# Dense bursts of four in three of eight half tiles, and the first tile turned two steps earlier

## The reference

```python
def attn(x):                     # 32 heads, KV_LAT = 4, HEAD_DIM = 32
    C_q, C_kv = x @ Wq_d + bq_d, x @ Wkv_d + bkv_d            # 12 and 4 columns
    q = (C_q @ W_qk + b_qk).reshape(b, s, 32, 4)
    scores = einsum('bqhd,bkd->bhqk', q, C_kv) / sqrt(4)
    V = (C_kv @ Wv_u + bv_u).reshape(b, s, 32, 32)
    out = einsum('bhqk,bkhd->bqhd', softmax(scores), V).reshape(b, s, 1024)
    return out @ Wo + bo
def ffn(x):                      # N = 8, RANK = 16
    h = einsum('bsd,nrd->nbsr', x, lora_A)
    return x @ W.T + bias + einsum('nbsr,nor->bso', h, lora_B * 2 * lora_weights)
x = x + attn(layernorm(x))
x = x + ffn(layernorm(x))
```

## Time and profile before

| | us |
|---|---|
| median of 3 runs | 2167.85 |
| the three runs | 2167.52, 2167.85, 2172.3 |
| the profiled execution | 2171.91 |
| its span | 2170.1 |
| preparation, up to the first scores | 137.7 |
| one of the chunks 2 to 6 | 243.0 |
| behind the last scores (2096.4) to the end | 73.7 |

### The profile page before, as it was taken

One profiled execution on the slowest core, in us unless ns is written; L12 is line 12 of the kernel. 1 busy time (PEld: TensorE's weight loads), 2 busy tenths in 40 slices (PEclk: granted clock), 3 DMA queues, 4 the chain that ended last, 5 costly groups with the idle time before them and its releaser, 6 DMA issues. The chain is left out here.

```text
span 2170.1 us, 35966 instructions
## 1 busy us (share of the span) xinstructions
PE 1954.2 (90%) x15023; PEld 717.3 (33%) x15023; DVE 511.2 (24%) x1292; ACT 2005.0 (92%) x2193; POOL 180.3 (8%) x100
## 2 busy tenths in 40 slices
PE   5748888799999999899999999899989999899989
PEld 3412222233333333233333333233333333233337
DVE  8732133212102110212102120212102120212125
ACT  6948999999999999999999999999999999999960
POOL 1210001000100001100100001100100000100111
PEclk9978999999999999999999999999999999999999
DMA  7432201000010000100010000100010000100010
GB/s 239 175 81 87 83 15 35 5 4 25 25 44 6 13 26 25 34 14 14 25 44 6 14 24 25 34 15 13 25 44 6 19 19 25 35 16 14 24 39 39
DMA packets 49116, 78.99 MB, mean 36 GB/s; under 512 B 17790, under 2 KB 33206, under 8 KB 48954
## 3 DMA queue, kind: packets, MB, share of 16 engines
q1 hardware_dynamic: 48954, 76.69, 10.6%
HBM read 52.02 MB, written 24.64 MB: 35 GB/s over the span
## 5 line engine op out<-in xcount | busy, mean ns | idle before, releaser
L554 ACT ACTIVATE probs<-ps 128x1024 f32<-128x1024 f32 x2048 | 1911.5, 1029 | 64.7 <-PE ps L765 37.9
L776 PE MATMUL ps<-probs,c_wide 128*32 128x512 f32 x8192 | 990.6, 601 | 0.0
L765 PE MATMUL ps<-q_in,key_t 30*128 30x512 bf16 x4096 | 405.2, 385 | 146.4 <-ACT probs L554 137.1
L821 PE MATMUL ps<-w_eff,xn_t 128*128 128x512 f32 x1344 | 387.0, 416 | 0.0
L765 PEld LDWEIGHTS ps<-q_in,key_t 30*128 30x128 bf16 x4096 | 103.8, 91 | 766.5 <-ACT probs L554 712.0
L776 PEld LDWEIGHTS ps<-probs,c_wide 128*32 128x32 f32 x8192 | 213.3, 109 | 427.3 <-issue 241.3
L1230 DVE TENSOR_TENSOR y<-ps,y 128x512 f32<-128x512 f32 x64 | 44.3, 692 | 965.2 <-PE ps L821 954.9
L821 PEld LDWEIGHTS ps<-w_eff,xn_t 128*128 128x128 f32 x1344 | 230.4, 188 | 98.5 <-issue 63.5
L460 POOL TENSOR_TENSOR y<-y,ffn_bias 128x1024 f32<-128x1024 f32 x32 | 76.2, 2381 | 1169.4 <-DVE xn L987 1169.4
L456 POOL TENSOR_TENSOR y<-y,attn_bias 128x1024 f32<-128x1024 f32 x32 | 76.2, 2383 | 704.8 <-DMA y<-in_L_attn_x_dram 704.6
L1009 DVE CAST xn_t<-ps 128x512 fp32r<-128x512 f32 x64 | 44.2, 691 | 158.9 <-PE ps L806 158.9
(11 more groups left out here) (130 smaller groups left out, 598.6 us busy)
## 6 DMA issues: line engine op xcount, KB each, us to landing
y<-in_L_attn_x_dram SPq DMA_DIRECT2D x48, 512.0 KB, 4.2
out_dram<-y SPq DMA_DIRECT2D x32, 512.0 KB, 2.7
area<-in_L_attn_x_dram SPq DMA_DIRECT2D x16, 512.0 KB, 4.5
q_in<-q_parts SPq DMA_DIRECT2D x256, 30.0 KB, 1.7
q_parts<-q_parts_sb SPq DMA_DIRECT2D x48, 128.0 KB, 2.1
y<-in_L_attn_Wo_dram SPq DMA_DIRECT2D x1, 2048.0 KB, 8.5
xn<-in_L_attn_Wo_dram SPq DMA_DIRECT2D x1, 2048.0 KB, 13.5
y<-in_L_ffn_W_dram SPq DMA_DIRECT2D x1, 2048.0 KB, 8.0
```

Source lines behind the costliest of these rows:

```text
L554: nc.scalar.activation(probs[:, (c * STEPS + step) % PROBS, bass.ts(pair, 2 * N)], ps[:, 2 * (i % SCORE_SLOTS):2 * (i % SCORE_SLOTS) + 2, ...
L765: last = nc.tensor.matmul(ps[:, at, :], key_t[TILE * h:TILE * h + KEYS, bass.ts(b * KT + kt, P)], q_in[TILE * h:TILE * h + KEYS, g % 2, :] ...
L776: last = nc.tensor.matmul(ps[32 * h:32 * h + 32, SUMS, :], c_wide[:, b * KT + kt, at:at + 32], probs[:, (c * STEPS + step) % PROBS, bass.t ...
L821: last = nc.tensor.matmul(ps[:, SHARED, :], xn_t[:, t % 2, a, kb, :], w_eff[:, b, kb, bass.ts(half, N)], start=(kb + i == 0), stop=(kb == ...
```

## The change

The plan is now computed, from a table of burst sizes per tile and half. Sizes of 4 give six bursts, sizes of 5 give five. The high halves of tiles 0, 1 and 2 have size 4; all others stay at 5. The first tile starts at step 13, which is `FIRST_AT + 6`. The computed steps are:

| tile | first turn | high bursts | next projections | low bursts |
|---|---|---|---|---|
| 0 before | 15 | 19 to 27 | 29, 31 | 33 to 41 |
| 0 after | 13 | 17 to 27 | 29, 31 | 33 to 41 |
| 1 before | 43 | 47 to 55 | 57, 59 | 61 to 69 |
| 1 after | 43 | 47 to 57 | 59, 61 | 63 to 71 |
| 2 before | 73 | 77 to 85 | 87, 89 | 91 to 99 |
| 2 after | 75 | 79 to 89 | 91, 93 | 95 to 103 |
| 3 before | 101 | 105 to 113 | none | 119 to 127 |
| 3 after | 105 | 109 to 117 | none | 119 to 127 |

`TURN_AT` goes from 71 to 73. `STORE_AT` and `LOAD_AT` keep their values.

```diff
-        DENSE_AT = (4, 6, 8, 10, 12, 18, 20, 22, 24, 26)
-        BURSTS = len(DENSE_AT) // 2
-        BURST = -(-3 * KB // BURSTS)
-        NEXT_AT = 14
-        TILE_STEPS = DENSE_AT[-1] + 2
+        BURST = ((4, 5), (4, 5), (4, 5), (5, 5))
+        BURSTS = [[-(-3 * KB // size) for size in sizes] for sizes in BURST]
         TURN_BACK_AT = BEHIND + 3
         FIRST_AT = BEHIND + 5
-        TILE_AT = [15, 15 + TILE_STEPS, 17 + 2 * TILE_STEPS, 17 + 3 * TILE_STEPS]
-        TURN_AT = TILE_AT[2] - 2
-        STORE_AT = [min(-(-(at + TILE_STEPS) // KT), G4 - 1) for at in TILE_AT]
+        TILE_AT, NEXT_AT, DENSE_AT = [], [], []
+        at = FIRST_AT + 6
+        for t in range(TT):
+            if t == 2:
+                TURN_AT = at
+                at += 2
+            TILE_AT.append(at)
+            high = [at + 4 + 2 * j for j in range(BURSTS[t][0])]
+            NEXT_AT.append(high[-1] + 2)
+            low = [high[-1] + 2 + (4 if t < TT - 1 else 0) + 2 * j for j in range(BURSTS[t][1])]
+            DENSE_AT.append((high, low))
+            at = low[-1] + 2
+        TILE_END = [low[-1] + 2 for high, low in DENSE_AT]
+        STORE_AT = [min(-(-at // KT), G4 - 1) for at in TILE_END]
...
             def dense_burst(p, t, half, j):
-                for kb, i in PRODUCTS[BURST * j:BURST * (j + 1)]:
+                size = BURST[t][half]
+                for kb, i in PRODUCTS[size * j:size * (j + 1)]:
...
-                    if at in DENSE_AT:
-                        half, j = divmod(DENSE_AT.index(at), BURSTS)
-                        if j == 0 and half == 0:
-                            pe.wait_ge(t_moved, START + CHUNKS * KB + (p * TT + t + 1) * 2)
-                        elif j == 0 and t < TT - 1:
-                            pe.wait_ge(y_ready, START + (p * TT + t + 2) * 2)
-                        elif j == 0:
-                            pe.wait_ge(ffn_moved, START + (p * TT + t) * 2 + 1)
-                        dense_burst(p, t, half, j)
+                    for half in range(2):
+                        if step in DENSE_AT[t][half]:
+                            j = DENSE_AT[t][half].index(step)
+                            if j == 0 and half == 0:
+                                pe.wait_ge(t_moved, START + CHUNKS * KB + (p * TT + t + 1) * 2)
+                            elif j == 0 and t < TT - 1:
+                                pe.wait_ge(y_ready, START + (p * TT + t + 2) * 2)
+                            elif j == 0:
+                                pe.wait_ge(ffn_moved, START + (p * TT + t) * 2 + 1)
+                            dense_burst(p, t, half, j)
```

More of the change, by code:

```diff
@@ L822, in dense_burst @@
                                             start=(kb + i == 0), stop=(kb == KB - 1 and i == 2))
-                if j == BURSTS - 1:
+                if j == BURSTS[t][half] - 1:
                     last.then_inc(ffn_ready, 1)
@@ L840, in dense_beside @@
                 for t in range(TT):
-                    at = step - TILE_AT[t]
-                    if at == 0:
+                    if step == TILE_AT[t]:
                         if t == 2:
@@ L847, in dense_beside @@
                         turn_xn(p, t, 0, SHARED)
-                    if at == 2:
+                    if step == TILE_AT[t] + 2:
                         pe.wait_ge(t_moved, START + CHUNKS * KB + (p * TT + t) * 2 + 1)
                         turn_xn(p, t, 1, SHARED)
-                    if t < TT - 1 and at == NEXT_AT:
+                    if t < TT - 1 and step == NEXT_AT[t]:
                         pe.wait_ge(ffn_moved, START + (p * TT + t) * 2 + 1)
                         project(p, t + 1, 0, SHARED)
-                    if t < TT - 1 and at == NEXT_AT + 2:
+                    if t < TT - 1 and step == NEXT_AT[t] + 2:
                         pe.wait_ge(y_ready, START + (p * TT + t + 1) * 2 + 1)
                         project(p, t + 1, 1, SHARED)
-                    if at in DENSE_AT:
-                        half, j = divmod(DENSE_AT.index(at), BURSTS)
-                        if j == 0 and half == 0:
-                            pe.wait_ge(t_moved, START + CHUNKS * KB + (p * TT + t + 1) * 2)
-                        elif j == 0 and t < TT - 1:
-                            pe.wait_ge(y_ready, START + (p * TT + t + 2) * 2)
-                        elif j == 0:
-                            pe.wait_ge(ffn_moved, START + (p * TT + t) * 2 + 1)
-                        dense_burst(p, t, half, j)
+                    for half in range(2):
[8 more added lines that the diff above has]
+                            dense_burst(p, t, half, j)
             def attention(c, b, b_before=None):
```

## The result

The changed kernel takes 2156.0 us (median of six runs, 2153.36 to 2157.92) against 2168.11 (six runs, 2167.51 to 2172.3). The ratio is 0.9942, with a 95% interval of 0.9931 to 0.9953. It is faster by 12.1 us. The forecast was a gain of 13.4 us and 2154.4 us.

The account below looks back on a forecast made before the run. ScalarE's exps were taken to pace light pairs, TensorE pairs with five dense matmuls. Saving 2.11 less 0.19 gives 1.92 us per chunk, 13.4 over 7 chunks: 2167.85 - 13.4 = 2154.4 us, range 2152.0 to 2160.5.

Parts of the forecast that it names:

- What sets the pace: In a pair of steps, ScalarE's four exps set 3.69 us up to four dense matmuls; with five, TensorE sets 3.866.
- A five costs 0.176: A pair whose odd step has five dense matmuls takes 0.176 us over the exps' pace; 12 fewer save 2.11 per chunk.
- the spare: In a pair with four dense matmuls, TensorE has about 0.05 us left before it would exceed the exps' pace.
- Light boundaries cost 0.095 each: Scores waiting for the next q_in behind light work add 0.095 us; steps 47 and 79 give back 0.19 per chunk.
- Sum 1.92 per chunk: Per chunk, 2.11 us saved on fives less 0.19 given back at boundaries; 13.4 us over 7 chunks.
- The moved waits: Turn at 13, tile 2's norm before the o_sb copy, tile 3's half-0 sum: 1.4, 1.4 and 1.7 us spare, no cost.
- TensorE's idle ahead of the scores: Idle before the score matmuls of L765 in a chunk, expected to fall from 14.3 us by about 2.
- The rival of the opening cost: Each burst shows 0.28 us in its pair; 21 more bursts take 5.9 us, gain 7.5, time 2160.4; chance 0.04.
- The rival of no change: TensorE's total work is the bound, or fours in a row use up their spare; 2167.9 us; chance 0.03.
- That of the wait at 13: TensorE stalls at tile 0's turn waiting for L987; losing a pair per chunk, 12.4 us slower, 2180.3; chance 0.03.

Follow-up runs that it names:

- The sixes: Changed kernel with the high halves of tiles 0, 1 and 2 as four bursts of six instead of six of four; 2206.72 us.
- the threes: Changed kernel with the high half of tile 2 as eight bursts of three and all other halves in fives; 2162.41 us.
- The turn at 11: Changed kernel with everything two steps earlier, the first tile's turn at step 11 and step 127 empty; 2173.66 us.
- The early turn alone: Changed kernel with the first turn kept at step 13 but all eight half tiles in 5+5+5+5+4; 2176.98 us.
- the run of two half tiles: Changed kernel with the first turn back at step 15 and only the high halves of tiles 0 and 2 in fours; 2160.16 us.
- the run of the same bursts two steps earlier: Changed kernel with the turn at 13, only the high halves of tiles 0 and 2 in fours, and step 127 empty; 2162.79 us.
- the run with the light steps at 113 to 117: Changed kernel with the turn at 13, all half tiles in fives, and tile 3's low half three odd steps later, ending at 127; 2168.47 us.

## Why the prediction was right

- **What sets the pace** was read rightly: ScalarE in pairs up to a four, TensorE from a five on. The sixes at 4.10 and the threes at 3.69 show both sides of it.
- **A five costs 0.176.** Fives stayed at 3.866. Fours, six on end, take 3.693 each, where the empty pairs of the changed kernel have a mean of 3.691: the spare was there.
- **Light boundaries cost 0.095 each.** The two new ones take 3.79, as the nearest row had it.
- **Sum 1.92 per chunk.** Measured 1.89 in each of chunks 2 to 6, and 13.5 us over chunks 1 to 7 against the 13.4 of the sum. That the two totals meet so closely is in part luck: seven chunks at 1.89 make 13.2, and the rest is that the fallen clock cost chunk 1 less after than before. A chunk has 15 fours more than before, and at 0.002 us each over an empty pair they make the 0.03 by which it missed.
- **The moved waits cost nothing**: 1.4, 1.4 and 1.7 us to spare, as worked out. The turn at 11 shows that the first is real: two steps earlier it stalls.
- **The median moved by 12.1 us, not 13.4.** The 1.3 us lie inside the interval of the ratio (10.2 to 15.0 us of gain, when its ends are applied to 2168.11) and stand against a scatter of nearly 5 us in the preparation and chunk 0.
- **Wrong in size**: TensorE's idle ahead of the scores fell by 3.2 us and not by about 2. The chunk became 1.9 us shorter, and TensorE's recorded busy time grew by 1.3 (228.70 to 230.01) at the same count of instructions, since its records overlap less; each filled pair loses all of its 1.11.
- **Left out**: that the place of the light steps matters for the clock. "The early turn alone" was forecast as no change by the same sum, and was 8.4 us slower than before. The changed kernel has no such fall in chunks 2 to 7, and its plan fills step 127; the prediction did not choose that for the clock's sake, so on this point it was right by luck. It also took 243.0 us for all seven chunks, where chunk 1 takes 244.7.

The rival of the opening cost fell with the threes and with the run of two half tiles. The rival of no change fell with the fours in a row. That of the wait at 13 has its mechanism shown, at step 11, where its condition is met.

## What to carry to other kernels

Find the smallest unit that repeats, here a pair of steps, and compare its start-to-start time with light and with heavy filling: that tells which engine sets it, and where the spare ends, which no busy share of the span does. Spread movable work so that no unit goes beyond the spare, and use empty slots for it before anything else. When work is moved forward, look at what becomes light behind it: light steps beside a wait can cost more through the clock than the move brings.

## What the runs showed of the hardware

Inside chunks 1 to 7 TensorE's granted clock fell to 0.50 (1.2 GHz) without any idle stretch over 2.3 us ahead of it. Before the falls at a chunk's start the engine had scores alone in step 127, 2.12 us of idle for the last exp, and step 1 empty behind it; before those in the chunk it had a stall of 2.26 us. The falls lasted 3.41 or 6.83 us, and the number of empty steps does not tell which: with one, they were of 6.83 us in the run with the turn at 11 and of 3.41 us in the run of the same bursts two steps earlier; with three, of both lengths. They struck some chunks of a run and not others, though TensorE's idle ahead of the change was 2.12 us in all of them; what decides it is not shown. A fall of 3.41 us cost 1.3 to 1.7 us and one of 6.83 us 2.6 to 2.7, and the light pair inside it took up to 5.45 us. Three empty odd steps in a row inside the chunk, with no wait for a last exp (the run with the light steps at 113 to 117), brought none.

The Trainium skill, page "TensorE: Matmul & The Clock Gate", section "Why this matters for your kernels", asks for no idle gaps over about 3 us between bursts of matmuls. By that rule none of these falls would be expected: the longest idle ahead of them was 2.26 us. Here the measurement decides: shorter waits beside light work were enough.
